# A state-space convolution in four chunks of 256 samples, joined by the modes of its kernel

## What is computed

```
mask = arange(1024) < length[:, None]
K    = 2 * real(einsum('hn,hnl->hl', Cs, exp(dtA[:, :, None] * arange(1024))))   # 64 modes a channel
y    = causal_convolution(x * mask, K) + x * mask * D          # for each batch and channel
x    = x + y * mask
x    = x + adapter(x, A1[id1], B1[id1])                        # rank 16, 8 adapters
x    = x + adapter(x, A2[id2], B2[id2])                        # rank 16, 64 adapters
x    = x + einsum('bct,bcd->bdt', x, W[id3]) + bias[id3]       # 32 subjects
```

## Time and profile before

| what | us |
|---|---|
| median of 3 runs | 754.1 (753.35 to 757.32) |
| profiled execution | 756.05 |
| its span, first to last instruction | 754.2 |
| TensorE matmuls busy | 715.3 (95%) |
| VectorE busy | 576.9 (76%) |
| ScalarE busy | 434.5 (58%) |
| GpSimd busy | 380.6 (50%) |

### The profile page before, as it was taken

One profiled execution on the slowest core, in us unless ns is written; L12 is line 12 of the kernel. 1 busy time (PEld: TensorE's weight loads), 2 busy tenths in 40 slices (PEclk: granted clock), 3 DMA queues, 4 the chain that ended last, 5 costly groups with the idle time before them and its releaser, 6 DMA issues. The chain is left out here.

```text
span 754.2 us, 19782 instructions
## 1 busy us (share of the span) xinstructions
PE 715.3 (95%) x6685; PEld 538.6 (71%) x6685; DVE 576.9 (76%) x1116; ACT 434.5 (58%) x760; POOL 380.6 (50%) x680
## 2 busy tenths in 40 slices
PE   2699999999999999999899999699999999999997
PEld 2377687787787787777677777477767777776774
DVE  7687987887886776876667665288888888888885
ACT  4535645645635636636335332277777777777775
POOL 1000088888885000047777200667676676767663
PEclk9799999999999999999999999899999999999999
DMA  6488989999899899899888982789999999999973
GB/s 209 119 277 246 325 281 335 282 362 332 293 368 359 273 356 337 292 311 296 288 249 269 321 291 118 297 272 315 315 311 323 315 324 316 319 320 319 317 259 154
DMA packets 121719, 219.97 MB, mean 292 GB/s; under 512 B 20226, under 2 KB 80194, under 8 KB 121666
## 3 DMA queue, kind: packets, MB, share of 16 engines
q1 hardware_dynamic: 102546, 166.56, 68.2%
q10 hardware_dynamic: 9904, 33.59, 11.6%
q0 software_dynamic: 9216, 19.15, 7.9%
HBM read 146.35 MB, written 72.91 MB: 291 GB/s over the span
## 5 line engine op out<-in xcount | busy, mean ns | idle before, releaser
L1078 PE MATMUL ps<-toep,xTh 128*128 128x512 f16 (+3 forms) x1024 | 210.3, 301 | 4.3 <-DMA diff<-d_rows 3.4
L1078 PE MATMUL ps<-toep,xTl 128*128 128x512 f16 (+3 forms) x512 | 147.4, 301 | 0.0
L1078 PEld LDWEIGHTS ps<-toep,xTh 128*128 128x128 f16 x1024 | 97.5, 98 | 56.5 <-DMA diff<-d_rows 4.3
L825 POOL DMA_INDIRECT gnow<-g_rows,idx_g x64 | 59.6, 931 | 115.9 <-DMA g_rows<-g_out 89.6
L801 POOL DMA_INDIRECT wnow<-in_L_cond_weights,idx_w x64 | 62.6, 978 | 100.7 <-DVEq L1015 83.6
L1271 POOL DMA_INDIRECT asel<-a_rows,idx_a x64 | 72.0, 1125 | 77.5 <-PE ps L1417 76.4
L1044 DVE TENSOR_TENSOR ps<-ps,common 128x512 f32<-128x512 f32 x64 | 44.6, 697 | 66.3 <-ACT common L867 66.0
L1266 POOL COPY bsel<-bt 128x256 f16 x256 | 92.7, 405 | 2.8 <-issue 2.2
L1356 DVE TENSOR_TENSOR xTl<-ps,xTh 128x1024 f16<-128x1024 f32 x64 | 78.4, 1224 | 13.6 <-ACT xTh L1315 10.3
L1078 PE MATMUL ps<-diff,xTh 128*128 128x256 f16 x512 | 87.3, 273 | 0.0
L217 DVE TENSOR_TENSOR xTl<-ps,xTh 128x1024 f16<-128x1024 f32 x64 | 77.7, 1214 | 0.0
(11 more groups left out here) (231 smaller groups left out, 1719.2 us busy)
## 6 DMA issues: line engine op xcount, KB each, us to landing
toep<-k_rows SPq DMA_DIRECT2D x64, 384.0 KB, 6.1
diff<-d_rows SPq DMA_DIRECT2D x64, 384.0 KB, 7.3
xt<-in_x SPq DMA_DIRECT2D x32, 512.0 KB, 6.4
x_rows<-xt ACTq DMA_DIRECT2D x32, 512.0 KB, 4.9
xt<-x_rows SPq DMA_DIRECT2D x32, 512.0 KB
out_dram<-outt SPq DMA_DIRECT2D x32, 512.0 KB, 7.9
out_dram<-diff SPq DMA_DIRECT2D x32, 512.0 KB
toep<-x_rows SPq DMA_DIRECT2D x24, 512.0 KB, 7.4
```

Source lines behind the costliest of these rows:

```text
L825: gp.indirect_dma_start(m.gnow[:, v, :], None, m.g_rows, bass.IndirectOffsetOnAxis(ap=m.idx_g[0:64, q:q + 1], axis=0)).then_inc(g_gathered ...
L1078: last = PE.matmul(out, xs[x_part], rhs(part), start=start and k == 0, stop=stop and k == 2)
```

## The change

The 1024 samples are cut in four chunks of 256. Within a chunk the convolution is done with Toeplitz tables as before (`within`). What earlier chunks add to a later one goes through a state: 64 complex modes, 128 real numbers for each batch. The state after a chunk is the turned samples times a table U (`ut`, the damped modes at 256 steps) plus the state before, rotated and damped by 256 steps (`rt`). The chunk's output gets the state times a table V (`vt`, the modes with their amplitudes at 256 steps). A channel has three states and, after each, three products from it.

Tables for a channel: `toep` is now 256 columns wide, `diff` is gone. U, V and the rotation matrices are computed for eight channels at a time, in two halves of four. U: ScalarE and VectorE make phases, sines and exponentials of 1024 columns from mode parameters that are stored to DRAM and loaded to all partitions (`load_modes`); VectorE multiplies the damping in (`wide_products`, L412), then high and low halves. V: the difference of two products, the first on VectorE (`v_first`, L442), the second on GpSimd (`v_second`, L452), joined on VectorE (`v_join`, L460). The rotation matrices are made on GpSimd (`turn_matrices`, L496).

After each state ScalarE copies the high half (`high_state`) and VectorE makes the low half (`low_state`). TensorE, one body, in the new order:

```diff
+                        if not (last and u == XU - 1):
+                            turn(i, u + 1)
+                        finish_high(i, u - 1)
+                        pe.wait_ge(m.toep_loaded[u % U], 16 * (2 * i + 1 + u // U))
+                            pe.wait_ge(low_ready, h)
+                        within(u, 0)
+                        state(i, u, 1)
+                        within(u, 1)
+                        from_state(i, u, 1).then_inc(low_done, 1)
+                            pe.wait_ge(x1_ready, h)
+                        within(u, 2)
+                        from_state(i, u, 2)
+                        state(i, u, 2)
+                        within(u, 3).then_inc(diag_done, 1)
+                        if not (last and u == XU - 1):
+                            state(i, u + 1, 0)
```

(`finish_high` stands for its two cases.) The new functions that it calls:

```diff
+                def state(i, u, n):
+                    out = state_bank(m, u, n)
+                    if n == 0:
+                        pe.wait_ge(m.xTl_ready, h + 1)
+                        if v % KP == 0:
+                            pe.wait_ge(m.u_ready, 2 * i + 1 + u // KP)
+                    for b in range(2):
+                        for k, (x_part, part) in enumerate(((m.xTh, 0), (m.xTl, 0), (m.xTh, 1))):
+                            last = PE.matmul(out, m.ut[:, b, v, part, :], x_part[:, u % 2, 2 * n + b, :], ...)
+                    if n:
+                        pe.wait_ge(m.s_ready, 3 * h + n)
+                        if n == 1 and v % KP == 0:
+                            pe.wait_ge(m.r_ready, 2 * (2 * i + v // KP + 1))
+                        for k, (part, before) in enumerate(((0, m.sh), (0, m.sl), (1, m.sh))):
+                            last = PE.matmul(out, m.rt[:, v, part, :], before[:, u % 2, n - 1, :], start=False, stop=(k == 2))
+                    last.then_inc(m.s_done, 1)
...
+                def from_state(i, u, c):
+                    pe.wait_ge(m.s_ready, 3 * h + c)
+                    if c == 1 and u % KP == 0:
+                        pe.wait_ge(m.v_ready, 2 * i + u // KP + 1)
+                    for k, (state, part) in enumerate(((m.sh, 0), (m.sh, 1), (m.sl, 0))):
+                        last = PE.matmul(out[:, first_col:first_col + SPAN], state[:, u % 2, c - 1, :], m.vt[:, u, part, :], ...)
```

GpSimd's queue of the channel stage:

```diff
-                gp.wait_ge(rows_ready, 1)
-                all_pairs(gather_w, keep_w, w_both)
-
-                gp.wait_ge(m.g_stored, 16 * G)
-                all_pairs(gather_g, keep_g, g_kept)
+                for i in range(TURNS):
+                    turn_matrices(nc, m, gp, i, 1)
+                    v_second(nc, m, gp, i, 1)
+                    if i == 1:
+                        gp.wait_ge(rows_ready, 1)
+                        for q in range(U):
+                            gather_w(q)
+                    if 1 <= i <= 5:
+                        w_unit(3 * i - 3)
+                    if i < TURNS - 1:
+                        turn_columns(nc, m, gp, i + 1)
+                        turn_matrices(nc, m, gp, i + 1, 0)
+                        if 1 <= i <= 5:
+                            w_unit(3 * i - 2)
+                        if i == 6:
+                            for k in range(0, 5):
+                                g_unit(k)
+                        v_second(nc, m, gp, i + 1, 0)
+                        if 1 <= i <= 5:
+                            w_unit(3 * i - 1)
+                        if i == 5:
+                            w_unit(15)
+                            gp.wait_ge(m.g_stored, 16 * G)
+                            for q in range(U):
+                                gather_g(q)
+                for k in range(5, PAIR_TURNS):
+                    g_unit(k)
```

More of the change, by code:

```diff
@@ L31 @@
 WARM = (33, 16, 12)
+S_SCALE = 64.0
 A_SCALE = 64.0
@@ new lines, in narrow_pairs @@
+def narrow_pairs(nc, m, act, k):
+    act.wait_ge(m.narrow_step, NARROW * k + 6)
+    for n, part in enumerate((m.ec, m.es)):
+        rows = slice(64 * n, 64 * n + 64)
+        nc.scalar.activation(m.ne[rows, :, 0:TB], part[rows, :, 0:TB], ACT.Copy).then_inc(m.pairs_ready, 1)
+    top, low = slice(0, 64), slice(64, 128)
+    act.wait_ge(m.rc_step, 2 * k)
+    for rows, n, src, sign in ((top, 0, m.ec, 1.0), (top, 1, m.es, 1.0), (low, 0, m.es, -1.0), (low, 1, m.ec, 1.0)):
+        nc.scalar.activation(m.rc[rows, :, n:n + 1], src[rows, :, 2 * TB:NT], ACT.Copy, scale=sign * S_SCALE).then_inc(m.rc_ready, 1)
@@ new lines, in wide_products, with high_u @@
+def wide_products(nc, m, dve, k, e):
+    cut = slice(KP * e, KP * e + KP)
+    dve.wait_ge(m.wide_done, WIDE * k + WIDE)
+    dve.wait_ge(m.u_ready, 2 * k + e)
+    for n, part in enumerate((m.uc, m.us)):
+        nc.vector.tensor_tensor(m.pu[:, :, :, n, :], part[:, :, cut, :], m.ue[:, :, cut, :], ALU.mult).then_inc(m.pu_ready, 1)
+def high_u(nc, m, act, k, e, first=False):
+    act.wait_ge(m.pu_ready, 4 * k + 2 * e + 2)
+    if not first:
+        act.wait_ge(m.s_done, 3 * (E * (k - 1) + KP * e + KP))
+    nc.scalar.activation(m.ut[:, :, KP * e:KP * e + KP, 0, :], m.pu[:].rearrange("p b q s n -> p b q (s n)"), ACT.Copy).then_inc(m.u_high, 1)
@@ L404, in setup_stage @@
         nat_b = natural_b(m)
[L405 to L406 removed]
+        late = m.iwl[:].rearrange("p q n -> p (q n)").bitcast(F32)
+        nat_a, by_k = (late[:, n * L:(n + 1) * L] for n in (1, 2))
         at, a1c = transposed_a(m)
@@ L739, in body @@
                         if not (last and u > U):
-                            if not (first and u == 0):
-                                sp.wait_ge(conv_done, h)
                             if make_k and u == XU - 3:
@@ new lines, in state @@
+                    v = u % XU
+                    out = state_bank(m, u, n)
[3 more added lines that the diff above has]
+                            pe.wait_ge(m.u_ready, 2 * i + 1 + u // KP)
+                    for b in range(2):
+                        for k, (x_part, part) in enumerate(((m.xTh, 0), (m.xTl, 0), (m.xTh, 1))):
+                            last = PE.matmul(out, m.ut[:, b, v, part, :], x_part[:, u % 2, 2 * n + b, :],
+                                             start=(b == 0 and k == 0), stop=(n == 0 and b == 1 and k == 2))
@@ new lines, in state, with within @@
+                    if n:
[5 more added lines that the diff above has]
+                    last.then_inc(m.s_done, 1)
+                def within(u, c):
+                    out = conv_high if c >= 2 else conv_low
+                    first_col = SPAN if c % 2 == 0 else 0
+                    for j in range(2):
+                        for k, (x_part, part) in enumerate(((m.xTh, 0), (m.xTh, 1), (m.xTl, 0))):
+                            last = PE.matmul(out[:, first_col:first_col + SPAN - j * P], x_part[:, u % 2, 2 * c + j, :],
+                                             m.toep[:, u % U, part, j * P:SPAN], start=(j == 0 and k == 0), stop=(c == 0 and j == 1 and k == 2))
+                    return last
```

730 lines of the change are left out of this document (428 added, 302 removed).

## The result

The kernel of the change takes 883.63 us, the median of four runs (879.46 to 887.05), the kernel before beside it 755.71 (753.35 to 759.22): a ratio of 1.1686, 95% interval 1.161 to 1.1761. Slower was right, but by 17%, not by 5.6%; 883.6 lies far above the range of 756 to 832.

The account below looks back on a forecast made before the run. The prediction took TensorE, busy 95% of the span, as the bound. Its terms, -70 + 38 + 6 + 6 + 35 + 3 + 4 + 20 = +42, gave a median of 796 us, slower by 5.6%, range 756 to 832.

Parts of the forecast that it names:

- term 6: TensorE's clock: part of the time after one long pause and a few short ones runs at 1.2 GHz, +3 us.
- term 2: Channel stage: TensorE waits for the nearly full VectorE and for ScalarE's runs ahead of the states, +38 us (15 to 60).
- term 4: VectorE's two-SBUF-operand table operations meet GpSimd's: some five a turn at about 0.6 us, a third on the path, +6 us.
- Term 1: Channel stage: TensorE's own work falls to 5.17 us a channel and 10.6 us of waits go, -70 us.
- Terms 2 to 4: Channel stage: waits for VectorE and ScalarE +38, first turn's index setup no longer free +6, VectorE meeting GpSimd +6 us.
- third rival: VectorE and GpSimd lock each other in table operations: 40 us instead of 6, so 830 us; chance 0.15.
- Term 5: GpSimd's queue: v_second stands behind gather units and holds VectorE, 21.9 us of it in turn 6, +35 us.
- Term 7: Before the first convolution: VectorE has 8.1 us more to do, taken at the middle of its bounds, +4 us.
- Term 8: Stage's end: GpSimd's remaining units make the pause before the pair stage 26 us instead of 6, +20 us (4 to 24).
- The signs: Right: turn 6 pause some 22 us, GpSimd last by about 20. Wrong: channels at 5.2 throughout, or GpSimd's units not in the way.
- First rival: Slack between channel bodies absorbs the elementwise work, waits of 50 us fall to zero: 746 us, faster; chance 0.13.
- Second rival: GpSimd's gathers issue faster with less busy DMA engines, a G unit in 4.2 us: 772 us; chance 0.10.

Follow-up runs that it names:

- after: The kernel of the change itself, with no further edit, against the kernel before: 883.63 us, ratio 1.1686.
- the three edits: Kernel of the change with GpSimd's units behind its awaited product, adapter groups' steps moved earlier, and damping of U on GpSimd: 803.35 us, ratio 1.058.

## Why the prediction was wrong

Three steps failed. The clock was charged for one long pause (term 6, +3), and it took some 30 us. The adapter groups were charged for their instructions and not for a chain (term 2), and TensorE waited 34 us at `turn_a`. A third of the lock's price was put on the path (term 4, +6), and 18 us were.

- **Term 1, TensorE's own work (-70): right.** The last channels of the stage, with no tables to make, are 5.18 us apart (548.57 to 553.75) against 5.17, and TensorE waits for no Toeplitz table in after. Of the 10.6 us called "waits, mostly for tables", the trace before lists 7.1, and 3.4 of these behind a table. That "I let these 10.6 go too" holds only while the kernel is slow: with the three edits 11.7 us of waits for tables are back.
- **Terms 2 to 4, the flow (38 + 6 + 6 = 50): near in sum, wrong in one place.** Without `turn_a` (34.0) and some 32 for GpSimd's product (VectorE's waits, taken as passed on whole), the listed waits are 47. The step that failed is "5.5 with groups, where 3.1 us of TensorE work per four channels give cover". `turn_a` waits for VectorE's low half, behind `wide_fraction` in body 1 and behind `v_join` and the damping in body 5, and for ScalarE's ordering copy, behind the table load and the sines. The change put table work ahead of both. 5.2 and 3.4 us, four times each, 34 in all, and 45 with the clock.
- **Term 4, the lock (+6): too small.** With GpSimd's elementwise work cut, 18.0 us go. VectorE's instructions get 22.2 us shorter by it, 3.2 a turn, and "five meetings a turn at about 0.6 us" is 3.0: the meetings were sized about right. The step that failed is "a third of it on the path"; most of it is (18.0 of 22.2, with what the clock gives back). The third rival's 40 was too much. That terms 2 to 4 come near 50 is partly luck, since with 18 for the lock (its price with the three edits in) only some 30 of the 47 are left for the 44 of terms 2 and 3.
- **Term 5, GpSimd's queue (+35): right.** VectorE waited 32.2 us for the product, 22.8 of it in turn 6 (predicted 21.9), behind five G units; TensorE's wait there is 23.3.
- **Term 6, the clock (+3): far too small.** I took it for "one long pause and a few short ones". The clock fell 16 times in the stage and took some 30 us of work (the estimate above). With `turn_a`'s steps moved it fell less: TensorE is busy 682.4 us for the same 7645 matmuls instead of 695.6.
- **Term 7, the start (+4): 7.0.** The upper half of its bounds.
- **Term 8, the end (+20): 26.4.** GpSimd was last by 21 us, where the working had 26, and another 11 us passed from its last instruction to the next stage, for which the working had nothing. The two errors partly cancel.
- **The range.** 28 us of listed waits, 27 of the clock, 14 of short waits, 9 of start and end and 2 of the pair stage make 80, and the spans miss by 81. Most terms had bounds, but the clock had none and was tied to one pause, when it should have grown with the waits of terms 2 and 5.
- **The signs.** The pause of turn 6 and GpSimd as the last engine came as announced. "If channels take over 6.5 us while GpSimd computes, it is the lock" misleads: a turn with groups takes 69 us, over 8 a channel, and `turn_a` alone has 8.6 of them, the lock some 3.
- **First rival (the queues hide the table work):** false; cutting most of it saves 46.5 us even with the three edits. **Second rival (faster gathers):** false; they kept 0.90 and their gap of 0.30 at a DMA share of 0.42.

No version here that computes the whole result beats the kernel before. With the three edits the change is 5.8% slower, and with U and V not made after the first turn it is just level. What stays open: the 57 us above TensorE's floor in that kernel are only partly placed, and whether the Toeplitz loads at another place in SyncE's queue would give their 12 to 19 us back.

## What to carry to other kernels

When a change turns a full TensorE into one that waits, add what the clock takes to the waits: here 30 us beside 113 of listed waits, and 153 beside 288 where every pause was 4.4 to 4.9 us long. Look for the wait in steps that the change doesn't touch but now stands ahead of, since work added to an in-order queue delays whatever was placed at the end of a body. And give a shared queue its short, waited-for product before its long units: GpSimd's order was worth 44 us here, with the same instructions in the queue.

## What the runs showed of the hardware

- Behind a wait of 2.03 us TensorE ran some 3 us at half rate in one place (390.62) and at full rate in another (252.11). Behind 64 pauses of 4.4 to 4.9 us it lost 2.4 us of work each. With 42 increments spread over the channel the clock stayed at 1.00.
- A semaphore increment on TensorE's queue takes 0.1 us when nothing else is issued (42 in 4.4 us) and nearly hides between matmuls: 29.4 us for 2688 of them, 0.011 each.
- Where GpSimd was last, the next block of all engines began 11.0 us after its last instruction (11.01 in after and in two edited kernels, 10.95 behind ten us of elementwise work). In the kernel before, where TensorE was last, 2.4 us passed after its last filler product.
- A VectorE subtraction of 1024 elements took 1.20 to 1.22 us in after with an operand in PSUM, whatever GpSimd did, and up to 3.02 us with both in SBUF.
